# A pre-norm decoder layer on one core: the pair bodies written out, latents made in one piece, weighted sums and Y put next to other 32-column products, even maxima transposed into the second latents' bank

## What is computed

```python
x = x + self_attention(layernorm(x))          # 32 query heads of 16, 8 key/value heads, causal
# cross attention with latents
C_q  = Q @ Wq_d                               # 512 -> 64
C_kv = ctx @ Wkv_d                            # 1500 x 512 -> 1500 x 32, "latents"
q    = (C_q @ W_qk) -> 16 heads of 32
attn = softmax(q . C_kv / sqrt(32))           # 56*16 rows of 1500
x    = x + (attn @ (C_kv @ Wv_u))
x    = x + (x_n @ kernel + bias + LoRA(x_n))  # LoRA factors chosen by a gate
```

## Time and profile before

| | |
|---|---|
| median of 3 runs | 658.44 us (655.45 to 659.02) |
| profiled execution | 656.01 us, its span 654.2 us |
| granted PE clock, mean | 0.971 of full |
| busy: PE, PEld, DVE, ACT, POOL | 585.3, 313.5, 431.8, 302.9, 415.8 us |

### The profile page before, as it was taken

How to read it: one execution, slowest core, us unless ns; L and a number is a source line. 1 busy time by engine, 2 the same in 40 slices (tenths; PEclk the granted TensorE clock), 3 DMA queues, 4 the chain that set the end, 5 groups by cost and what they waited for, 6 DMA issues and landing times.

```text
span 654.2 us, 13476 instructions
## 1 busy us (share of the span) xinstructions
PE 585.3 (89%) x4144; PEld 313.5 (48%) x4144; DVE 431.8 (66%) x715; ACT 302.9 (46%) x642; POOL 415.8 (64%) x385
## 2 busy tenths in 40 slices
PE   6778797898999899998999899998999899988887
PEld 6325443364456355364446355464456355434445
DVE  2716885479657877479657867479657867556632
ACT  1430254337444565247444565347444565465460
POOL 5001185488776896498776896498767897788000
PEclk8897898699999999999999999999999999999899
DMA  8939710650118310580118310670128310200000
GB/s 330 395 68 347 229 37 22 232 218 20 27 44 278 166 44 20 188 283 20 27 46 295 147 44 23 214 254 22 24 55 290 143 44 23 58 23 1 24 1 15
DMA packets 31589, 77.54 MB, mean 119 GB/s; under 512 B 11297, under 2 KB 24961, under 8 KB 29218
## 3 DMA queue, kind: packets, MB, share of 16 engines
q1 hardware_dynamic: 30882, 75.27, 34.4%
q10 hardware_dynamic: 640, 1.39, 0.6%
HBM read 58.92 MB, written 2.88 MB: 94 GB/s over the span
## 4 chain that ended last, share of the span: by engine, by line
PE 63%; DVE 17%; issue 6%; ACT 6%; POOL 4%; DMA 2%; SPq 1%; ACTq 0%; DVEq 0%; POOLq 0%
PE st_ps L731 11%; PE mx_ps L774 9%; PE pv_ps L746 9%; PE mi_ps L516 5%; DVE mx_p L1152 4%; PE mi_ps L523 4%; PE mi_ps L510 4%; POOL acc L1225 3%; PE mi_ps L709 2%; PE mi_ps L606 2%; PE mi_ps L610 2%; DVE p L1116 2%; PE mi_ps L713 2%; ACT p_ring L948 2%; DVE xn L1027 2%
## 5 line engine op out<-in xcount | busy, mean ns | idle before, releaser
L1225 POOL TENSOR_TENSOR acc<-acc,p_ring 125x448 f32<-125x448 f32 x290 | 350.7, 1209 | 53.3 <-ACT p_ring L948 29.2
L1152 DVE TENSOR_REDUCE mx_p<-mx_ps 128x1 f32<-128x500 f32 x336 | 209.9, 668 | 105.7 <-PE mx_ps L774 104.6
L948 ACT ACTIVATE p_ring<-st_ps 125x448 f32<-125x448 f32 x372 | 183.4, 543 | 161.1 <-PE st_ps L731 139.9
L731 PE MATMUL st_ps<-q_st,c_st 98*125 98x448 f32 x372 | 145.2, 430 | 12.4 <-ACT p_ring L948 6.8
L774 PE MATMUL mx_ps<-c_st,q_st 96*128 96x500 f32 x336 | 140.3, 449 | 13.8 <-DVE p L1075 4.8
L731 PEld LDWEIGHTS st_ps<-q_st,c_st 98*125 98x125 f32 x372 | 66.2, 189 | 102.7 <-ACT p_ring L948 75.1
L746 PE MATMUL pv_ps<-p_ring,c_nat 125*32 125x448 f32 x768 | 95.8, 562 | 3.6 <-issue 1.7
L1233 POOL TENSOR_TENSOR rstd<-mv,eps_col 128x1 f32<-128x1 f32 x24 | 4.5, 189 | 138.3 <-DVE mv L1023 137.8
L774 PEld LDWEIGHTS mx_ps<-c_st,q_st 96*128 96x128 f32 x336 | 62.6, 194 | 45.9 <-issue 23.1
L523 PE MATMUL mi_ps<-ctx_sb,wkv_sb 128*32 128x375 f32 x480 | 47.8, 519 | 2.1 <-DVE p L1075 2.0
L1225 POOL TENSOR_TENSOR acc<-p_ring 125x448 f32<-125x448 f32 x29 | 35.8, 1235 | 16.5 <-ACT p_ring L948 16.5
(11 more groups left out here) (136 smaller groups left out, 669.8 us busy)
## 6 DMA issues: line engine op xcount, KB each, us to landing
ctx_sb<-in_ctx_t SPq DMA_DIRECT2D x16, 3000.0 KB, 11.2
c_st<-ct_hl SPq DMA_DIRECT2D x192, 46.9 KB, 2.3
q_st<-q_hl SPq DMA_DIRECT2D x90, 56.0 KB, 2.0
x_sb<-in_x SPq DMA_DIRECT2D x8, 256.0 KB, 2.7
out_y<-x3n SPq DMA_DIRECT2D x16, 112.0 KB
wq_sb<-in_wq SPq DMA_DIRECT2D x2, 512.0 KB, 5.5
kern_sb<-in_lora_a SPq DMA_DIRECT2D x1, 1024.0 KB, 13.9
wo_sb<-in_wo SPq DMA_DIRECT2D x1, 1024.0 KB, 18.9
```

The lines of the kernel that those rows point to most:

```text
L731: mm(st_bank(unit)[0:KC, 0:HALF], c_st[:, b % 4, t * KT + k * KC:t * KT + (k + 1) * KC], q_st[:, b // 2 % 2, b % 2, half * HALF:(half + 1) ...
L948: act.activation(p_ring[:, unit % PR, :], st_bank(unit)[0:KC, 0:HALF], ACT.Exp, scale=float(L) ** -0.5).then_inc(exp_done, 1)
L1152: ve.tensor_reduce(mx_p[:, p:p + 1], mx_ps[unit % MXB][:, 0:KP], AX.X, ALU.max).then_inc(red_done, 1)
L1225: po.tensor_tensor(dst, first, p_ring[:, unit % PR, :].rearrange("p (h s) -> p h s", s=S), ALU.add).then_inc(acc_done, 1)
```

## The change

First, all nine bodies are written out; every wait compares with a constant, and the register arithmetic ahead of waits is gone. Second, Ah and A follow each other with nothing between. Third, in groups 0, 7 and 8 the weighted sums come after the fourth S, next to the latents, to O1 or to DN, and Y comes right behind O1. Fourth, the even maxima are no longer transposed between Ah and A into a bank of their own but behind A, into columns 384 to 511 of the bank that holds the latents; on ACT SE0 moves behind the copies of both. V no longer waits for the copy of the maxima but for the mask additions. Fifth, on ACT the copy of the finished sums in group 6 moves behind the copy of P1.

```diff
 STEPS = [
-    [("Ah", "a"), ("M", 2), ("L0", "n"), ("M", 1), ("A", "a"), ("AS", "a"), ("N0", "n")],
+    [("Ah", "a"), ("A", "a"), ("M", 2), ("L0", "n"), ("M", 1), ("AS", "a"), ("N0", "n")],
...
-    [("SE0", "n"), ("Ah", "b"), ("MT", "m"), ("A", "b"), ("SE1", "n"), ("V", "n"), ("SN0", "n")],
+    [("Ah", "b"), ("MT", "m"), ("A", "b"), ("SE0", "n"), ("V", "n"), ("SE1", "n"), ("SN0", "n")],
...
-    [("O1", "n"), ("M", 3), ("Y", "f")],
+    [("O1", "n"), ("Y", "f"), ("M", 3)],
...
+LATE_SUMS = (0, 7, 8)
...
-        def run_bodies(eng, at, body):
+        def run_bodies(body):
-            body(0)
-            with eng.Fori(0, (LAST_LOOPED - FIRST_LOOPED + 1) // LOOP_BODIES) as rnd:
...
-            for i in range(LAST_LOOPED + 1, PAIRS + 1):
+            for i in range(PAIRS + 1):
                 body(i)
...
+            def turn_maxima(b):
+                pe.wait_ge(nm_step, 3 * b + 3)
+                pe.transpose(mi_ps[1][0:2 * ROWT, KG * 128:(KG + 1) * 128],
+                             nm_hl[:, :, :].rearrange("p a j -> p (a j)").bitcast(F32), ident[:, :])\
+                    .then_inc(ps["MT"], 1)
...
                 elif name == "V":
-                    if n:
-                        pe.wait_ge(mt_sb, due(mt_sb, 2 * n - 1))
+                    pe.wait_ge(s1_sb, 4 * n + 4)
...
                 elif name == "A":
-                    last = latents(o, slot, (2, 3))
+                    latents(o, slot, (2, 3)).then_inc(ps[name], 1)
+                    if n % 2 == 0 and n:
+                        turn_maxima(n - 2)
+                    return
...
                 elif name == "Y":
+                    if n + 2 == PAIRS:
+                        pe.wait_ge(mt_sb, B - 1)
...
-                        if t == 1 and 0 <= bl < B:
+                        if t == (3 if g in LATE_SUMS and bm < B else 1) and 0 <= bl < B:
                             sums(bl, gl)
...
                     bl, gl = (bs, gg - 1) if gg else (bs - 1, GROUPS - 1)
-                    if 0 <= bl < B and gl % KG == KG - 1:
+                    behind = "P1" if g == GROUPS and i + 1 < PAIRS else None
+                    if 0 <= bl < B and gl % KG == KG - 1 and not behind:
                         out_of_sums(bl, gl // KG)
                     for name, n in steps_of(i, g):
                         step(name, n, i, g)
+                        if name == behind and 0 <= bl < B:
+                            out_of_sums(bl, gl // KG)
```

More of the change, by code:

```diff
@@ L256, in decoder_layer @@
[L256 to L288, removed]
+        x_in = [sem(f"x_in{n}") for n in range(2)]
+        ctx_in = [sem(f"ctx_in{n}") for n in range(2)]
+        ab_in = sem("ab_in")
+        w_attn = sem("w_attn")
+        w_out = sem("w_out")
+        w_latent = sem("w_latent")
+        w_cross = sem("w_cross")
+        w_ffn = sem("w_ffn")
+        raw_in = sem("raw_in")
@@ new lines, in decoder_layer @@
+        eff_out = sem("eff_out")
+        cst_in = [sem(f"cst_in{n}") for n in range(4)]
+        m_in = [sem(f"m_in{n}") for n in range(2)]
+        q_in = [[sem(f"q_in{n}_{t}") for t in range(4)] for n in range(2)]
+        y_out = sem("y_out")
+        pool_c = sem("pool_c")
+        dve_c = sem("dve_c")
+        gk_done = sem("gk_done")
+        lora_ps = sem("lora_ps")
+        lora_sb = sem("lora_sb")
+        ln = [sem("ln0"), sem("ln1"), sem("ln2")]
+        ln_eps = [sem(f"ln_eps{n}") for n in range(3)]
@@ L290, in decoder_layer @@
+        x3_base = sem("x3_base")
+        ln_pow = [sem(f"ln_pow{n}") for n in range(3)]
+        st_done = sem("st_done")
+        exp_done = sem("exp_done")
+        pv_done = sem("pv_done")
+        ox_sb = sem("ox_sb")
+        acc_done = sem("acc_done")
+        acc_dve = sem("acc_dve")
+        mx_done = sem("mx_done")
+        red_done = sem("red_done")
+        nm_step = sem("nm_step")
         ps = {}
@@ L293, in decoder_layer @@
                 continue
[L294 to L319, removed]
+            ps[name] = sem("ps_" + name)
+        t1_sb = sem("t1_sb")
+        k_sb = sem("k_sb")
+        v_sb = sem("v_sb")
+        q1_sb = sem("q1_sb")
+        s1_sb = sem("s1_sb")
+        soft = sem("soft")
+        soft_e = sem("soft_e")
+        soft_n = sem("soft_n")
+        pt_sb = sem("pt_sb")
+        o1_sb = sem("o1_sb")
+        t2_sb = sem("t2_sb")
+        cq_sb = sem("cq_sb")
+        qh_hi = sem("qh_hi")
+        qh_lo = sem("qh_lo")
+        a_f = sem("a_f")
+        a_hi = sem("a_hi")
+        a_lo = sem("a_lo")
+        ct_sb = sem("ct_sb")
+        mt_sb = sem("mt_sb")
+        yu_sb = sem("yu_sb")
+        dn_sb = sem("dn_sb")
+        r_sb = sem("r_sb")
+        t3_sb = sem("t3_sb")
+        f1_sb = sem("f1_sb")
+        f2_sb = sem("f2_sb")
         def step_bank(name, n):
@@ L425, in store_y @@
             def store_y(n):
[L426 removed]
+                sp.wait_ge(f2_sb, n + 1)
                 for h in range(2):
[L428 removed]
+                    dma(out[n, h], x3n[h * SLOT:h * SLOT + S, :]).then_inc(y_out, 16)
             load_x(0)
@@ L495, in body @@
                 if i == 0:
-                    sp.wait_ge(eff_out, due(eff_out, 32))
-            run_bodies(sp, at, body)
-            sp.wait_ge(y_out, due(y_out, 32 * PAIRS + 16))
+                    sp.wait_ge(eff_out, 32)
+            run_bodies(body)
+            sp.wait_ge(y_out, 32 * PAIRS + 16)
         @block.tensor
         def _(pe):
-            at = [None]
-            due = counter(at)
             mm = pe.matmul
@@ L838, in body @@
                 if i == 0:
-                    pe.wait_ge(w_ffn, due(w_ffn, 16 * 3))
-                    pe.wait_ge(y_out, due(y_out, 16))
-            run_bodies(pe, at, body)
+                    pe.wait_ge(w_ffn, 16 * 3)
+                    pe.wait_ge(y_out, 16)
+            run_bodies(body)
         @block.scalar
         def _(act):
-            at = [None]
-            due = counter(at)
             def copy(dst, src, scale=1.0):
@@ L1025, in normalise @@
             def normalise(which, n, src, dst):
-                ve.wait_ge(ln_pow[which], due(ln_pow[which], n + 1))
+                ve.wait_ge(ln_pow[which], n + 1)
                 ve.tensor_scalar(dst, src, mv[:, which, 0:1], rstd[:, which, 1:2], ALU.subtract, ALU.mult)\
@@ L1143, in add_up @@
                     else:
-                        ve.wait_ge(acc_dve, due(acc_dve, dve_adds(b, half) + k - 1))
+                        ve.wait_ge(acc_dve, dve_adds(b, half) + k - 1)
                         first = dst
@@ L1198, in body @@
                         step(name, n, i, g)
-            run_bodies(ve, at, body)
+            run_bodies(body)
         @block.gpsimd
         def _(po):
-            at = [None]
-            due = counter(at)
             def add_up(b, half, since=1, until=ADDS):
@@ L1244, in make @@
                 instruction.then_inc(pool_c, 1)
-                po.wait_ge(pool_c, due(pool_c, made[0]))
+                po.wait_ge(pool_c, made[0])
             make(po.memset(ident[:, :], 0.0))
@@ L1292, in body @@
                 add_up(2 * i, 1, since=4)
-            run_bodies(po, at, body)
+            run_bodies(body)
 def kernel(**inputs):
```

315 lines of the change are left out of this document (138 added, 177 removed).

## The result

The changed kernel takes 672.07 us (median of 4 runs, 671.50 to 672.54) against 657.64 for the kernel before, measured beside it. The ratio is 1.0218, 95% interval 1.0194 to 1.0242. The predicted 657.5 us was too low, and the time lies outside the range of 644 to 662.

A forecast was written before the change was run, and what follows sets the result against it. PE, busy 585.3 of 654.2 us, was taken to bound the kernel through its sequence and waits. Bodies 1 to 6 +4.0, body 0 +1.3, body 7 -0.5, loop -4.7 gave +0.1 us; forecast 657.5, no change, range 644 to 662.

The forecast's parts named there:

- loop written out: Both jumps back to the loop's start go, -4.7 us; the register arithmetic was taken at nothing.
- bodies 1 to 6: group 0: Groups 0 and 1: L0 and N0 come later, T1 waits 1.4 us, each body is 1.10 us behind.
- groups 4 to 8, by rows: V's and P2's waits go and visits are saved, but ACT and DVE leave 0.44 us saved a body.
- body 0: Same chain as group 0 in the other bodies, first latents partly at half clock: +1.3 us.
- body 7: No layer norm and no T1, so it keeps group 0's saving less what DVE holds back: -0.5 us.
- what groups 7 and 8 save: 0.73 us saved by group 8, then its seven M wait for DVE's reductions at 0.59 us each, leaving 0.44.
- the one on groups 4 to 6: V 0.85 us early, SE0's move on ACT takes back half; group 5's exponentials start at 373.45, 0.42 saved.
- The clock: Rival: a 1.4 us wait at T1 or group 5 halves the clock, 1.3 to 2 us a body, 668; chance 0.12.
- The signs named beforehand: Wrong if T1's wait is under 0.7 us, period under 72.3, or clock below 1.00 between 140 and 550 us.

The follow-up runs named there:

- the loop alone: The kernel before with all bodies written out and nothing else changed: 651.23 us, ratio 0.9908.
- the fill: The changed kernel plus seven products nobody reads, behind the sums of group 5 in bodies 1 to 6: 667.19 us, ratio 1.0151.
- the two late rows mended: The changed kernel with SE0 first in group 4 and L0 and N0 ahead of group 0's three M: 654.20 us, ratio 0.9939.
- the last four: Changed kernel, old group 0, SE0 first: 655.22 us; instead L0, N0, SE0 ahead: 654.20; that with old groups 7, 8: 649.12; written-out kernel before, group 0 changed, L0, N0 ahead: 648.65.

## Why the prediction was wrong

The sum of the prediction, term by term, in spans (us):

```
term                      forecast  measured  read from
loop written out             -4.7      -6.2   648.0 - 654.2
bodies 1 to 6: group 0       +6.6      +7.2   6 x (73.09 - 71.89)
  groups 4 to 8, by rows     -2.6      +2.5   6 x ((71.97 - 71.89) + (73.48 - 73.15))
  groups 4 to 8, by clock     0        +8.9   6 x (74.96 - 73.48)
body 0                       +1.3      +3.5   (199.55 - 192.95) - 3.07
body 7                       -0.5      -0.4   (669.7 - 574.71) - (648.0 - 552.63)
sum                          +0.1     +15.5   spans: 669.7 - 654.2 = 15.5
```

(552.63 and 192.95 are F2 of bodies 6 and 1 with the loop alone; 3.07 is 74.96 - 71.89. The two terms of groups 4 to 8 come from different kernels, so how they share the 11.4 is less sure than their sum. The sizes are those of the profiled executions; by the medians group 0 costs more, 9.5, and the fill gives less, 4.9.)

**Right.** Group 0: "the body is 1.10 us behind", 1.20 measured, by the chain described, though T1 waited 1.02 us and not 1.4, since PE itself came later. V lost its wait, as forecast. And what groups 7 and 8 save does meet DVE's reductions: with the two late rows mended, the M of group 8 run at DVE's 0.58 us. Nothing of the saving is left there, and outside the middle bodies this part of the change cost 5.1 us by the medians, which the forecast did not have.

**The step that failed** is the one on groups 4 to 6: "V starts at 370.25", "SE0's move takes back half. I take the exponentials' start at 373.45, 0.42 saved." With the 1.10 of group 0 that made 374.55, and it was 375.33. Of the 0.78, 0.48 is V's: the latents waited 0.52 us for DVE's mask adds. The loop alone has that wait too (0.51), the kernel before not, so the new order of the steps did not make it. In these two DVE's small cast ahead of the mask adds runs beside POOL's additions, in the kernel before POOL pauses there. DVE's timeline of body 4, before:

```profile
365.83 0.17 DVE L1163 CAST nm_hl<-nm 128x7 fp32r<-128x7 f32 x1
```

and in the changed kernel:

```profile
376.40 0.76 DVE L1134 CAST nm_hl<-nm 128x7 fp32r<-128x7 f32 x1
```

The other 0.30 is the row of ACT, 3.50 us from V to the exponentials instead of the 3.20 I allowed. The net gain was counted as half of V's lead. It should have been counted by laying out the row itself: m_t, ct_f, SE0, vhat, SE1, one behind the other. Everything in it was in the trace of before except its new order. V's lateness delays PE as well, so of the 0.78 only the row's 0.30 lengthens PE's wait; PE itself got from V to the wait in 2.35 us instead of 2.46. So it was 1.74 instead of the forecast 1.3, and that brought in the second failure.

**The clock** was a rival with its price about right ("1.3 to 2 us a body, some +10"; 1.48 and 8.9 measured) and its chance of 0.12 too low; the sum had it at nothing. I had waits up to 0.91 us without a fall (the trace has one of 1.12 too, behind the first jump) and one of 2.02 with it, and put two waits of 1.4 between these. At group 5 the 0.4 us of error decided it: behind 1.74 us the clock fell in all six bodies, behind 1.29 in one. The clock is the largest term, 8.9 of the 15.5 us. By this rival I had 668; the rest is in the other rows of the table.

**The loop** was undersized: I priced the jumps from the trace and took the register arithmetic at nothing. Each body was 0.33 us shorter as well. It comes behind Wh: from Wh to H PE takes 10.39 us instead of 10.55, and from H to the end of the body 10.97 instead of 11.15. That it is the hand-overs between engines there is argued, not tested.

**Body 0** lost 3.5 us, where I had 1.3. Over the first 150 us the granted clock is 0.86, with the loop alone 0.91. The kernel without the change of group 0 is 0.86 there and 2.9 us late at the end of body 1, the one without the change of groups 7 and 8 is 0.89 and 1.5 us late. So groups 7 and 8 have a part in it. These are single traces, and the cause of the longer falls stays open.

**The signs named beforehand.** T1's wait (1.02, above 0.7, though under the 1.2 to 1.6 expected) and the period (74.96, above 72.3) stayed clear of the bounds set for being wrong, though the period was 2.1 us over the forecast. The clock did not: it was to stay at 1.00 between 140 and 550 us, and it fell in every body.

**Still open:** why the period settles at 71.9 to 72.0 us in five kernels (the loop alone and the last four) in which V's start differs by 0.8 us. In the two with V at 30.35 an M of group 7 waits 0.65 us for DVE's reductions (body 4), and Wh comes no earlier than with the loop alone. No run relieves DVE there.

## What to carry to other kernels

A step that leaves PE's order as it is can still cost PE: after moving an instruction, write out the whole row of the engine that issues it, up to the one that PE waits for, and look at its idle time (SE0 fitted into 2.7 us of it and was taken out). When a forecast wait comes near one that has lowered the clock elsewhere in the trace, give the fall a real chance, price it in full, and look at a run before trusting the wait's length alone. A group of products that is joined to save visits pushes everything behind it: find the latest consumer (here the norm), and move what feeds it ahead first.
